# Two P transfers, one v transfer: a new issue order for SP, with a new table of steps on five engines

## The reference

```python
for i in range(6):
    x = attn_layer(shift_tokens(x), Wqkv[i], q_scale[i], k_scale[i], Wo[i]) + x
    x = ffn_layer(shift_tokens(x), ln_g[i], ln_b[i], W1[i], b1[i], W2[i], b2[i]) + x

def attn_layer(x, Wqkv, qs, ksc, Wo):            # 16 heads of 64
    q, k, v = split(x @ Wqkv, 3)
    q, k = rotary(l2norm(q) * qs), rotary(l2norm(k) * ksc)
    # windows of 32 tokens; each sees itself and the window before
    attn = softmax(where(mask, -max, 8 * q @ k2.T))
    return (attn @ v2) @ Wo

def ffn_layer(x, ...):                            # 128 -> 2*341 -> 128
    a, gate = split(layernorm(x) @ W1 + b1, 2)
    return a * gelu(gate) @ W2 + b2
```

## Time and profile before

| | |
|---|---|
| median of three runs | 3517.3 us |
| the profiled execution | 3534.39 us |
| its span | 3532.6 us |
| granted TensorE clock, mean over the span | 0.976 |
| PE busy | 3108.0 us, 88% |
| DVE busy | 2935.2 us, 83% |
| POOL busy | 2429.1 us, 69% |
| ACT busy | 2115.4 us, 60% |
| DMA busy | q1: 36.3% of 16 engines |

### The profile page before, as it was taken

One profiled execution on the slowest core, in us unless ns is written; L12 is line 12 of the kernel. 1 busy time (PEld: TensorE's weight loads), 2 busy tenths in 40 slices (PEclk: granted clock), 3 DMA queues, 4 the chain that ended last, 5 costly groups with the idle time before them and its releaser, 6 DMA issues.

```text
span 3532.6 us, 118084 instructions
## 1 busy us (share of the span) xinstructions
PE 3108.0 (88%) x50214; PEld 2417.3 (68%) x50214; DVE 2935.2 (83%) x3356; ACT 2115.4 (60%) x2794; POOL 2429.1 (69%) x1229
## 2 busy tenths in 40 slices
PE   7889898899988999888887898998898898898888
PEld 5767777777777777765333677777777677677777
DVE  6878888887888888886998888888888888888885
ACT  5556556565566556557776556555565565565655
POOL 6767677676676776662998768667667667667663
PEclk8999999999999999999999999999999999999999
DMA  3434344344344443431100434434434434434432
GB/s 112 119 97 106 104 108 117 98 113 118 96 110 119 106 108 92 103 97 31 39 0 13 119 90 106 123 90 111 122 96 108 122 95 104 116 99 107 106 88 80
DMA packets 247413, 343.41 MB, mean 97 GB/s; under 512 B 41005, under 2 KB 139886, under 8 KB 246894
## 3 DMA queue, kind: packets, MB, share of 16 engines
q1 hardware_dynamic: 246894, 335.85, 36.3%
HBM read 35.80 MB, written 1.05 MB: 10 GB/s over the span
## 4 chain that ended last, share of the span: by engine, by line
PE 43%; SPq 25%; DMA 8%; issue 7%; DVE 7%; ACT 5%; POOL 4%; DVEq 0%; ACTq 0%; POOLq 0%
SPq L1995 15%; PE PS L427 12%; DMA ARENA<-PB 8%; SPq L1975 6%; PE PS L237 3%; PE PS L588 3%; PE PS L453 3%; PE PS L373 3%; PE PS L238 3%; PE PS L239 3%; SPq L1973 2%; PE PS L532 2%; PE PS L304 2%; PE PS L534 2%; PE PS L533 2%
## 5 line engine op out<-in xcount | busy, mean ns | idle before, releaser
L1821 POOL TENSOR_TENSOR ARENA<-ARENA 128x1024 f32<-128x1024 f32 x192 | 471.0, 2453 | 458.9 <-DVE ARENA L1388 457.7
L427 PEld LDWEIGHTS PS<-ARENA 128*64 128x64 f32 x12288 | 405.6, 146 | 241.8 <-DMA ARENA<-PB 181.6
L427 PE MATMUL PS<-ARENA 128*64 128x64 f32 x12288 | 435.9, 233 | 153.3 <-DMA ARENA<-PB 140.1
L1829 POOL TENSOR_TENSOR ARENA<-ARENA,RN 128x1024 f32<-128x1024 f32 x192 | 365.1, 1901 | 295.3 <-ACT RN L984 288.5
L237 PE MATMUL PS<-WL,XH 128*128 128x512 f32 x1152 | 512.4, 445 | 44.9 <-DVE ARENA L1388 34.7
L1063 ACT ACTIVATE ARENA<-PS 128x1024 f32<-128x1024 f32 x192 | 196.3, 1023 | 515.0 <-PE PS L427 515.0
L304 PE MATMUL PS<-C,ARENA 128*128 128x128 f32 x3120 | 410.8, 277 | 94.9 <-issue 63.9
L238 PE MATMUL PS<-WH,XL 128*128 128x512 f32 x1152 | 461.8, 401 | 0.0
L239 PE MATMUL PS<-WH,XH 128*128 128x512 f32 x1152 | 461.4, 401 | 0.0
L1815 POOL TENSOR_TENSOR ARENA<-ARENA 128x1024 f32<-128x1024 f32 x192 | 455.3, 2371 | 7.0 <-DVE ARENA L1370 7.0
L304 PEld LDWEIGHTS PS<-C,ARENA 128*128 128x128 f32 x3120 | 348.8, 142 | 132.6 <-issue 102.1
(11 more groups left out here) (166 smaller groups left out, 6446.8 us busy)
## 6 DMA issues: line engine op xcount, KB each, us to landing
ARENA<-ARENA SPq DMA_DIRECT2D x576, 256.0 KB, 4.2
ARENA<-PB SPq DMA_DIRECT2D x1488, 64.0 KB
ARENA<-ARENA SPq DMA_DIRECT2D x384, 128.0 KB, 2.7
ARENA<-in_wqkv SPq DMA_DIRECT2D x36, 512.0 KB, 4.8
ARENA<-in_wo SPq DMA_DIRECT2D x12, 512.0 KB, 4.0
ARENA<-in_w SPq DMA_DIRECT2D x12, 341.0 KB, 4.2
ARENA<-in_w SPq DMA_DIRECT2D x12, 192.0 KB, 4.6
QKS<-in_qks SPq DMA_DIRECT2D x12, 128.0 KB, 2.4
```

The source lines that it names most:

```text
L427: last = nc.tensor.matmul(out.rearrange("p (a q) -> p a q", a=2)[:, :, col:col + 32], v2[:, win, hp, :], pt[:, :, win, hp, :], start=True, ...
L1821: nc.gpsimd.tensor_tensor(KN[n % 2], KN[n % 2], T2, ALU.add).then_inc(k_add, 1)
```

## The change

It has three parts.

1. **SP's order.** `spread_probs` is gone. `spread_values(n)` now calls `probs_of(n - 1, win)`, two P transfers for each window, ahead of each v transfer: P P, the tail of v, v, P P, v, P P, v, P P, v. The first P transfer's waits now stand ahead of all v transfers. The tail, which reads the v of the tile before, has a semaphore of its own (`tail_in`), and `v_evacuate` waits for that tail and for the v transfers of two tiles before, no longer for all v transfers of the tile before.
2. **PSUM bank of `out_project`.** Bank 6 (in the slot of the scores) in place of bank 2. `out_project` therefore waits for `sub_done` of the tile before, `scores` and `ffn_up1` wait for `res_done`, and `k_transpose` does so no longer.
3. **The table of steps.** The lists of PE, ACT, DVE and POOL have a new order.

```diff
@@ scores
                 if (s - 24) % 4 == 3:
                     after_chunk(pe, f_h[1], (s - 24) // 4)
-                after_tile(pe, sub_done, s - 21)
+                after_tile(pe, res_done, s - 23)
@@ spread_ready, new; called by values
+            def spread_ready(n):
+                pe.wait_ge(tail_in, 16 * (n0 + n + 1))
+                pe.wait_ge(v2_in[n % 2], 64 * ((n0 + n) // 2 + 1))
@@ out_project
-                after_tile(pe, car_ev, s - 20)
+                after_tile(pe, sub_done, s - 21)
...
-                out_products(n, 2)
+                out_products(n, 6)
@@ PE's list
                 k_project(s - 19)
+                k_transpose(s - 20)
+                q_transpose(s - 20)
                 out_project(s - 23)
-                q_transpose(s - 20)
-                k_transpose(s - 20)
...
+                ffn_centre(s - 23)
+                carry(s - 19)
+                bias_products(s - 20)
                 scores(s - 20)
-                bias_products(s - 20)
-                carry(s - 19)
-                ffn_centre(s - 23)
+                ffn_variance(s - 23)
                 ffn_down(s - 24)
                 values(s - 22)
-                ffn_variance(s - 23)
@@ v_evacuate
                 if n:
-                    act.wait_ge(v2_in[(n - 1) % 2], 80 * ((n0 + n - 1) // 2 + 1))
+                    act.wait_ge(tail_in, 16 * (n0 + n))
+                if n >= 2:
+                    act.wait_ge(v2_in[n % 2], 64 * ((n0 + n) // 2))
@@ POOL's list
                 k_add_halves(s - 18)
                 p_normalise(s - 20)
-                w_low_k(s - 18)
+                k_normalise(s - 18)
                 q_normalise(s - 18)
                 q_add_halves(s - 17)
-                k_normalise(s - 18)
@@ spread_values and probs_of
+                probs_of(n - 1, 0)
                 last, v = (VT[i % 2].rearrange("p (a c) -> p a c", a=2) for i in (n - 1, n))
-                sp.dma_start(v2[0:64, 0, :], last[96:128, :, :]).then_inc(v2_in[n % 2], 16)
+                sp.dma_start(v2[0:64, 0, :], last[96:128, :, :]).then_inc(tail_in, 16)
                 sp.dma_start(v2[64:128, 0, :], v[0:32, :, :]).then_inc(v2_in[n % 2], 16)
                 for win in range(1, 4):
+                    probs_of(n - 1, win)
                     sp.dma_start(v2[:, win, :], v[32 * win - 32:32 * win + 32, :, :]).then_inc(v2_in[n % 2], 16)
...
             for n in range(N):
                 spread_values(n)
-                spread_probs(n - 1)
```

More of the change, by code:

```diff
@@ L165, in build @@
         w1_in, inw_in, mw_in = sem("w1_in"), sem("inw_in"), sem("mw_in")
-        v2_in = [sem(f"v2_in{i}") for i in range(2)]
+        v2_in, tail_in = [sem(f"v2_in{i}") for i in range(2)], sem("tail_in")
         eps_set, pad_set, zero_set, masks_set, edge_set, tab_set, floor_set = (sem(n) for n in (
@@ L329, in k_transpose @@
                     pe.wait_ge(b_add, n // NT + 1)
-                after_tile(pe, res_done, s - 23)
+                after_tile(pe, car_ev, s - 20)
                 if (s - 25) % 4 == 3:
@@ L333, in k_transpose @@
                 if (s - 24) % 4 == 3:
+                    after_chunk(pe, f_ln, (s - 24) // 4)
                     after_chunk(pe, f_xm, (s - 24) // 4)
@@ L1876, in pool_stack @@
                     low_input(3)
+                w_low_k(s - 18)
                 ffn_low(s - 23)
```

72 lines of the change are left out of this document (34 added, 38 removed).

## The result

The changed kernel takes 3334.95 us (median of four runs, 3328.84 to 3341.26). The kernel before takes 3517.24 us on the same chip (3502.58 to 3526.32). The ratio is 0.9486, with a 95% interval of 0.9448 to 0.9523: 182 us less, where 217 were forecast. The profiled execution took 3337.3 us, its span is 3334.8 us, and the mean granted clock is 0.984.

A forecast was written before the change was run, and what follows sets the result against it. SP's loop of thirteen issues, P landing and `values` bounds plain steps; PE bounds the FFN step. 13.1 + 14.5 + 19.8 + 12.8 = 60.2, plus 1.1 is 61.3 against 66.1 a group; 46 x 4.8 = 221 us less: 3300, range 3225 to 3460.

The forecast's parts named there:

- The loop of SP: Plain step: last P transfer twelfth issue, landing 10.1 us after the first with 0.97 of 2.01 still held; loop 12.3 us.
- The rule against it: Trainium skill's 435 GB/s between SBUF and SBUF: a v transfer takes 0.60 us, no backlog forms, only one issue is gained.
- The plain step, 13.1: DVE becomes the bound: 14.02 without its 1.11 us of waiting is 12.9, plus 0.2 for hidden waits.
- The centre step, 14.5: Variance product moves in ahead of `values`; PE work of 13.40 + 1.1 bounds the step, against 14.54 now.
- the step behind the FFN step, 12.8: DVE's work is the plain step's size but starts with slack from the FFN step: 12.8 us, against 13.07.
- The FFN step, 19.8: Loses 1.1 us of PE work and the 0.97 wait behind `o_evacuate`; 19.3 plus 0.5 of waiting, against 21.87.
- The surplus, 1.1: A group's time beyond its four steps, 2.6 us, falls to 1.1: slow clock and late landings mostly go, layer loads stay.
- POOL, "costs nothing": `k_normalise` first on POOL closes a longer loop through DVE, about 12.9 us, just under 13.1, so it costs nothing.
- Rival A: SP's order gains only one issue, 0.64 us, since v does not cause the holding: -106 us, 3410; 15%.
- B: Last P lands later, each P pair queuing behind a v transfer; loop 15.0 us, slower by 92 us, 3610; 9%.
- C: New loop through POOL outlasts DVE's own; `q_add_halves` ends late and `k_rotate2` waits on DVE: -92 us, 3425; 10%.
- D: The table makes some step wait unseen: no change, or slower by up to 100 us; 6%.

## Why the prediction was right, and where it was off

The forecast case came about, 35 us short of the number. Point by point:

- **The loop of SP.** Right as to the landing and the holding; what the holding was worth was not. The last P was to land 10.1 us after the first issue, with 0.97 us still held. `values` begins 10.1 us after it; 0.61 is held by that step's issues. The part of the holding that was put to the burst of v is gone, and the single long issue stayed, as the split of the 2.01 us said. That the long one is a cause of its own is supported by the thin v transfers, in which it is still there. But SP's order alone gave only 65 us, and in the old table the turns gave no time over one v transfer behind P. A likely reason, from the waits and not from a test, is that PE met its next waits, for ACT (43.7 us) and for its own instructions (75.8).
- **The rule against it.** By the Trainium skill, page DMA: Bandwidth & Descriptors, section Where 436 GB/s comes from, a 256 KB transfer takes an estimated 0.60 us, so three of them in a row could hold nothing up. The runs do not agree: eight P issues behind the tail and three v transfers took 5.74 and 6.86 against 5.08 undisturbed, while the first three P pairs in turn with v took 1.19, 1.25 and 1.35, against 1.24 undisturbed.
- **The plain step, 13.1.** In the quiet group it is 12.29, better than said. DVE is busy 12.14 of it, where 12.62 were busy before, but PE is busy 12.05: the forecast that DVE alone would bound it is half right, and SP is released by PE. The mean over the first stack is 13.7, in which PE idles 1.25, 0.46 of it in stops inside `values` and 0.36 for the landing of P, and DVE 0.58.
- **The centre step, 14.5, and the step behind the FFN step, 12.8.** 14.37 and 13.79 in the quiet group, 14.48 and 12.93 in the mean. The numbers are right. The second was put to DVE, but DVE idles 1.5 us of it in the mean, almost all for ACT, and PE 0.95, so that number is in part luck.
- **The FFN step, 19.8.** 19.20 in the quiet group, median 19.5. The variance was priced at 1.1 + 0.97; moving it back costs 1.9 in that step and gives 0.3 in the centre step. Right, except for one wait that was not seen: that `out_project` finds its input ready is true of ACT's part, but it also waits for `sub_done` now, 3.2 to 3.9 us in each of the two last FFN steps of either stack.
- **The surplus, 1.1.** This is the term that was mis-sized. It was expected that slow clock and late landings go and "the loads of a layer stay", so the surplus of 2.6 would fall to 1.1. It is still 61.9 - 59.65 = 2.3. Late landings did mostly go (PE's wait for P is 33 us against 140). But PE's stops for its own instructions, 11 and 14.4 us before, are now 52 and 93.4 us. They weigh most in the FFN steps at a layer's beginning: the eight of the two stacks have a mean of 24.0 us, 4.5 over the median, where before they had 22.2, 0.7 over the usual 21.5. The loads were booked as a constant that stays, without asking what they would cost on a PE that waits for nothing else. With them thinned the time is 29 us lower, which is most of the 35 us that were missing; the waits for `sub_done` in the last layer are another 14.5. That the total still comes so near is in part luck, since the quiet group is 0.55 better than the sum.
- **POOL, "costs nothing".** Right of the change, but too little was said. The estimated loop of 12.9 leaves POOL waits of 0.17 and 0.79 in a plain step that takes 12.29, so that loop is shorter than was estimated. The order on POOL is not a convenience, though: without it the new list of PE costs 376 us. The prediction followed POOL's own loop and not who stands behind `k_transpose` on PE.
- **Rival A, only one issue gained.** Wrong as to the time (3410), half right as to SP: one v transfer behind P does all that turns do in the old table and nearly all in the new one. Its doubt whether the holding is v's doing is answered: behind a burst of v the first two P issues are held by 0.75 to 0.79 us in the mean, in turn with v by at most 0.07. The order's gain lies mainly in the issue and in the landing that is no longer last, and the table decides how much of it is used: 65 us with the old one, 159 with the new (3493.7 against 3334.95).
- **Rivals B, C and D.** B and C did not come: P lands no later, and DVE waits 2.6 us in all for L1820. Of D, a wait made by the table or the bank that was not seen, there is a little, the 14.5 us for `sub_done`. A wait of PE for `res_done` is not among its larger ones.

What stays open: why a packet of instructions begins late when large transfers run. The trace has when it begins and ends, not when it was asked for, so it does not tell a request that stands behind data from one that was made late. What of the 93.4 us of such stops lies on the path that sets the time was not measured either.

## What to carry to other kernels

Two changes can be worth little apart and much together when each ends at a wait that the other removes, so test the pair before dropping the halves. A moved step has to be followed to the instructions that now stand behind its input on every engine, not only along its own loop. When an engine becomes the bound, large loads that were free beside idle time get a price on it: spread them over steps, and look for idle time without a releaser in the middle of long blocks of small instructions. Where a profile names no releaser, lay the end of the stop beside the ends of other things: here it lay a constant time behind an instruction packet in 52 cases, and behind an operation of DVE in seven.

## What the hardware showed that was not expected

PE stops between two products of one block, without a semaphore, after the same 98th product of `scores` in two kernels: for 1.27 us when little is being moved and 3.73 us behind three loads of 512 KB. Such stops end 1.21 to 1.59 us after the end of a 16 KB packet of the instruction queue, in 52 of 59 cases; without the loads the packet begins 1.1 us before the stop, with them 1.2 us after its beginning. PE was in such stops for 14.4 us before the change, when it waited for P, and for 93.4 us after it. After the long stop the granted clock was 0.54 in the next 5.43 us, after the short one `ffn_down` ran at its full speed (2.85 us). Issuing P ahead of all v was slower by 61 us than taking turns, though PE's wait for P had gone: the v transfers in a row then met PE's products, and its stops in `values` went from 63.0 to 114.0 us.
